# GpSimd makes the angle and decay tables of an S5 block; VectorE keeps the step chain; rotation products are summed in PSUM

## The reference

```python
x_in = x
x = groupnorm(x, groups=32)                 # over 3 channels x 256 positions
u = x.reshape(16, 96, 256).transpose(0, 2, 1)
fx = layernorm(u) * ln1_g + ln1_b           # over the 96 channels
lam = Lambda[:, 0] + 1j * Lambda[:, 1]      # 48 modes
step = exp(log_step)
mask = step * abs(Lambda[:, 1]) / (2 * pi) < 0.25
lam_bar = exp(lam * step)
B_bar = ((lam_bar - 1) / lam)[:, None] * Bc
xs[l] = lam_bar * xs[l-1] + B_bar @ fx[l]   # along the 256 positions
y = 2 * real((Cc * mask) @ xs) + D * fx
y = gelu(y) + fx
fy = layernorm(y) * ln2_g + ln2_b
z1, z2 = split(fy @ W_enc.T)
out = x_in + (z1 * gelu(z2)) @ W_dec.T + fy
```

## Time and profile before

| | us |
|---|---|
| three runs | 110.3, 112.12, 112.47 |
| their median | 112.12 |
| the profiled execution, its own time | 110.42 |
| its span, first to last instruction | 108.6 |
| TensorE matmul busy | 94.9 (87%) |
| VectorE busy | 77.6 (71%) |
| ScalarE busy | 41.0 (38%) |
| GpSimd busy | 31.9 (29%) |

### The profile page before, as it was taken

The page is one execution under the profiler, slowest core; times in us unless marked ns, Lnnn a source line. Parts: engine busy times, 40 slices in busy tenths (PEclk is TensorE's granted clock), DMA queues, the critical chain, the costliest instruction groups (busy, mean ns, idle before and its releaser), DMA issues.

```text
span 108.6 us, 1488 instructions
## 1 busy us (share of the span) xinstructions
PE 94.9 (87%) x502; PEld 56.2 (52%) x502; DVE 77.6 (71%) x260; ACT 41.0 (38%) x79; POOL 31.9 (29%) x26
## 2 busy tenths in 40 slices
PE   5999897269989929999899999999599999999960
PEld 4668766146555715676476655567324432533310
DVE  1688999999986899658677302389990289994590
ACT  2254167807449100024037009818049722024200
POOL 8600000400049992000018000007995000296000
PEclk9999999955799999999999999999999999999997
DMA  2997000000000000000000000000000000450135
GB/s 77 275 262 168 3 0 0 6 0 0 0 0 0 0 0 3 0 6 0 0 0 0 0 0 3 6 0 0 0 0 0 0 0 0 118 149 29 28 84 177
DMA packets 3767, 3.79 MB, mean 35 GB/s; under 512 B 496, under 2 KB 3664, under 8 KB 3760
## 3 DMA queue, kind: packets, MB, share of 16 engines
q1 hardware_dynamic: 3392, 3.49, 12.3%
q10 hardware_dynamic: 368, 0.20, 0.8%
HBM read 2.12 MB, written 1.57 MB: 34 GB/s over the span
## 4 chain that ended last, share of the span: by engine, by line
PE 70%; DVE 21%; issue 4%; ACT 1%; DVEq 1%
PE ps L424 70%; DVE st L836 2%; DVE fy L664 2%; DVE pm L885 2%; DVE sc L694 2%; DVE rs L664 1%; DVE upper L668 1%; DVE sq L664 1%; DVE tb L664 1%; DVE tb L668 1%; DVE y L982 1%; DVE gn L664 1%; DVE rs L694 1%; DVE fx L664 1%; DVE sc L664 1%
## 5 line engine op out<-in xcount | busy, mean ns | idle before, releaser
L424 PE MATMUL ps<-fy,mt 96*96 96x512 f32 x32 | 14.9, 600 | 1.3 <-DVE fy L664 1.3
L290 POOL TENSOR_TENSOR y<-gl,fx 96x512 f32<-96x512 f32 x4 | 6.1, 1524 | 29.8 <-ACT gl L379 29.8
L298 POOL TENSOR_TENSOR res<-fy,xs 96x512 f32<-96x512 f32 x8 | 10.7, 1359 | 11.6 <-DVE fy L664 11.5
L424 PE MATMUL ps<-xs,pm 96*96 96x256 f32 x32 | 10.8, 492 | 3.3 <-DVE pm L885 3.3
L385 ACT ACTIVATE y<-ps,vecs 96x512 f32<-96x512 f32 x8 | 5.5, 687 | 16.4 <-PE ps L424 16.4
L664 DVE SCALAR_TENSOR_TENSOR w<-ps,vecs,y 96x512 f32<-96x512 f32 x8 | 5.9, 743 | 7.4 <-ACT y L385 7.4
L424 PE MATMUL ps<-fx,dm 96*96 96x512 f32 x16 | 8.4, 605 | 2.6 <-issue 2.2
L933 DVE TENSOR_TENSOR Z<-Z,ps 96x240 f32<-96x240 f32 (+3 forms) x8 | 2.8, 355 | 9.5 <-PE ps L424 9.5
L424 PEld LDWEIGHTS ps<-fy,mt 96*96 96x96 f32 x32 | 5.0, 163 | 8.7 <-issue 6.8
L424 PEld LDWEIGHTS ps<-xs,pm 96*96 96x96 f32 x32 | 6.4, 214 | 5.9 <-DVE pm L885 3.8
L379 ACT ACTIVATE gl<-ps,db 96x512 f32<-96x512 f32 x8 | 5.5, 684 | 9.4 <-PE ps L424 9.4
(11 more groups left out here) (112 smaller groups left out, 168.1 us busy)
## 6 DMA issues: line engine op xcount, KB each, us to landing
out_dram<-sq SPq DMA_DIRECT2D x8, 192.0 KB, 2.2
xs<-x_dram SPq DMA_DIRECT2D x3, 384.0 KB, 6.1
xs<-x_dram SPq DMA_DIRECT2D x2, 192.0 KB, 3.5
mt<-mats_dram SPq DMA_DIRECT2D x1, 338.6 KB, 6.8
mt<-mats_dram ACTq DMA_DIRECT2D x1, 180.0 KB, 3.9
sm<-small_dram ACTq DMA_DIRECT2D x1, 8.6 KB, 2.8
cmask<-mask_dram ACTq DMA_DIRECT2D x1, 9.0 KB, 4.9
```

The source lines that it names most:

```text
L290: nc.gpsimd.tensor_tensor(yv[:, RT * i:RT * (i + 1), :], cols(gl, H, i).rearrange("c (b m) -> c b m", b=RT), cols(fx, H, i).rearrange("c ( ...
L298: nc.gpsimd.tensor_tensor(cols(res, H, i), cols(fy, H, i), xs[:, HB * H + 2 * i:HB * H + 2 * i + 2, :].rearrange("c n l -> c (n l)"), ALU. ...
L424: return nc.tensor.matmul(o, lhsT, rhs, start=start, stop=stop)
```

## The change

`parameters()` and `output_tables()` are gone from VectorE. In their place VectorE has `step_chain()`, the part up to TH and RE, which ends in `angle_unit_ready`; it also makes DEN and ABSI. Its steps are laid two behind each statistic of the first half. The order of VectorE between the statistics and the first layernorm is rewritten: no parameter steps stand inside `group_norm` and `inverse_sigma` any more, the statistics of half 1 stand between the `scale_centering` of half 0, and at the end a new `input_bias()` makes the bias column of `bst`.

GpSimd makes everything from ANG and XK on: angle reduction, `expm1_table`, cosine and sines, `bst`, and then the output tables, `db` and `dm`. A step that was one `scalar_tensor_tensor` on VectorE is two instructions there. `rotT` is replaced by `rotC` and `rotS`, both made whole on GpSimd. TensorE multiplies `bst` by both and sums the two in PSUM: four matmuls for two. `yl` is combined before `rotX`. TensorE has fourteen more warm-ups ahead of `center_batch(1, 0)`. The removed functions are left out here, and are in the code above.

```diff
-WARM = (10, 2, 14)
+WARM = (10, 2, 14, 14)
 WARM_N = 256
-FIRST_PM = 4
 ...
+            def expm1_table(p, y, q, arg):
+                settle()
+                ts(y, arg, 1 / 128, -80 / 128, ALU.mult, ALU.max)
+                settle()
+                ts(p, y, 1 / 120, None, ALU.mult)
+                for c in (1 / 24, 1 / 6, 1 / 2, 1.0):
+                    settle()
+                    ts(q, p, c, None, ALU.add)
+                    settle()
+                    tt(p, q, y, ALU.mult)
+                for _ in range(7):
+                    settle()
+                    ts(q, p, 2.0, None, ALU.add)
+                    settle()
+                    tt(p, q, p, ALU.mult)
+            pool.wait_ge(in_small, 16)
+            pool.wait_ge(angle_unit_ready, 2)
+            ts(tbl(ANG), s(KV, NK), scol(TH), None, ALU.mult)
+            ts(tbl(XK), s(KV, NK), scol(RE), None, ALU.mult)
+            settle()
+            ts(tbl(NRND), tbl(ANG), 1 / (2 * np.pi), ROUND, ALU.mult, ALU.add)
+            settle()
+            ts(tbl(NRND), tbl(NRND), -ROUND, None, ALU.add)
+            for part in (TWO_PI_HI, TWO_PI_MID, TWO_PI_LO):
+                settle()
+                ts(tbl(RED), tbl(NRND), -float(part), None, ALU.mult)
+                settle()
+                tt(tbl(ANG), tbl(RED), tbl(ANG), ALU.add)
+            settle()
+            nc.gpsimd.tensor_scalar(tbl(RED), tbl(ANG), PI_BELOW, -PI_BELOW, ALU.min,
+                                    ALU.max).then_inc(angles_ready, 1)
+            expm1_table(tbl(EXM), tbl(TMP), tbl(RK), tbl(XK))
+            pool.wait_ge(sines_ready, 2)
+            tt(tbl(SH2), tbl(SH), tbl(SH), ALU.mult)
+            ts(tbl(NSS), tbl(SIN), s(RHO), None, ALU.mult)
+            settle()
+            ts(tbl(CM1), tbl(SH2), -2.0, None, ALU.mult)
+            ts(tbl(RK), tbl(EXM), 1.0, None, ALU.add)
+            settle()
+            ts(tbl(COS), tbl(CM1), 1.0, None, ALU.add)
+            pool.wait_ge(in_mats, 16)
+            pool.wait_ge(den_ready, 1)
             nc.gpsimd.tensor_tensor(
-                rotT[:, :, :], m(M_ID).unsqueeze(1).broadcast_to([96, T, 96]),
-                tbl(COS, T).unsqueeze(2).broadcast_to([96, T, 96]), ALU.mult).then_inc(rotcos_ready, 1)
-            pool.wait_ge(in_mats, 16)
+                rotS[:, :, :], m(M_SW).unsqueeze(1).broadcast_to([96, T, 96]),
+                tbl(NSS, T).unsqueeze(2).broadcast_to([96, T, 96]), ALU.mult).then_inc(rot_ready, 1)
+            settle()
+            nc.gpsimd.tensor_tensor(
+                rotC[:, :, :], m(M_ID).unsqueeze(1).broadcast_to([96, T, 96]),
+                tbl(COS, T).unsqueeze(2).broadcast_to([96, T, 96]), ALU.mult).then_inc(rot_ready, 1)
+            tt(tbl(RSIN), tbl(RK), tbl(SIN), ALU.mult)
+            tt(scol(T1), tbl(EXM, 1, 1), tbl(COS, 1, 1), ALU.mult)
+            settle()
+            tt(scol(T3), tbl(RSIN, 1, 1), s(LI), ALU.mult)
+            tt(scol(T1), scol(T1), tbl(CM1, 1, 1), ALU.add)
+            settle()
+            tt(scol(T4), scol(T1), s(LI), ALU.mult)
+            ts(scol(CRE), scol(T1), s(LR), scol(T3), ALU.mult, ALU.add)
+            settle()
+            ts(scol(CIM), tbl(RSIN, 1, 1), s(LR), scol(T4), ALU.mult, ALU.subtract)
+            tt(scol(CRE), scol(CRE), scol(DEN), ALU.mult)
+            settle()
+            ts(scol(CIM), scol(CIM), scol(DEN), s(RHO), ALU.mult, ALU.mult)
+            settle()
+            ts(bt1[:, :], m(M_BS), scol(CIM), None, ALU.mult)
+            ts(bst[:, 0:C], m(M_B), scol(CRE), None, ALU.mult)
+            settle()
+            nc.gpsimd.tensor_tensor(bst[:, 0:C], bst[:, 0:C], bt1[:, :], ALU.add).then_inc(bst_ready, 1)
+            ts(tbl(SSG), tbl(SIN), s(NRHO), None, ALU.mult)
+            settle()
+            tt(tbl(RSSG), tbl(RK), tbl(SSG), ALU.mult)
+            settle()
+            tt(scol(ABSI), scol(ABSI), scol(STEP), ALU.mult)
+            settle()
+            ts(scol(MASK), scol(ABSI), float(np.float32(2 * np.pi)) / 4, 2.0, ALU.is_lt, ALU.mult)
+            settle()
+            tt(scol(MR), scol(MASK), s(NRHO), ALU.mult)
+            ts(scol(MI), scol(MASK), -1.0, None, ALU.mult)
+            settle()
+            ts(tbl(CU), tbl(COS), scol(MR), None, ALU.mult)
+            ts(tbl(SU), tbl(SIN), scol(MI), None, ALU.mult)
+            for dst, unit in ((XCO, COS), (XSI, SSG)):
+                ts(tbl(dst, 1, 0), tbl(unit, 1, T), tbl(RK, 1, 1), tbl(RK, 1, 0), ALU.mult, ALU.mult)
+                ts(tbl(dst, 1, 1), tbl(unit, 1, K16), tbl(RK, 1, 1), tbl(RK, 1, T), ALU.mult, ALU.mult)
+                tt(tbl(dst, 4, 2), tbl(unit, 4, K16), tbl(RK, 4, K16), ALU.mult)
+            nc.gpsimd.tensor_tensor(db[:, :], s(DD), s(B1), ALU.mult).then_inc(db_ready, 1)
+            nc.gpsimd.tensor_scalar(dm[:, :], m(M_ID), s(DD), None, ALU.mult).then_inc(dm_ready, 1)
+            settle()
 ...
-            pool.wait_ge(tables_ready, 1)
+            combine(yl, M_C, tbl(CU, T), M_CS, tbl(SU, T), T).then_inc(yl_ready, 1)
             combine(rotX, M_ID, tbl(XCO, NX), M_SW, tbl(XSI, NX), NX).then_inc(rotx_ready, 1)
-            combine(yl, M_C, tbl(CU, T), M_CS, tbl(SU, T), T).then_inc(yl_ready, 1)
 ...
+            warm_up(WARM[3], bank(1, 0))
 ...
             pe.wait_ge(bst_ready, 1)
-            pe.wait_ge(rot_ready, T)
-            mm(bank(0, 2)[0:97, 0:480], bst[:, :], rotT[:, 0:5, :])
-            mm(bank(0, 3)[0:97, 0:288], bst[:, :], rotT[:, 5:8, :]).then_inc(umat_done, 1)
+            pe.wait_ge(bias_col_ready, 1)
+            pe.wait_ge(rot_ready, 2)
+            for part, first, last in ((2, 0, 5), (3, 5, 8)):
+                o = bank(0, part)[0:97, 0:96 * (last - first)]
+                mm(o, bst[:, :], rotS[:, first:last, :], stop=False)
+                last_mm = mm(o, bst[:, :], rotC[:, first:last, :], start=False)
+            last_mm.then_inc(umat_done, 1)
 ...
+            def step_chain():
+                norm.next_stt(scol(REC), s(LS), -1.0, s(LS), ALU.mult, ALU.max)
+                norm.add(nc.vector.tensor_tensor(scol(T2), s(LR), s(LR), ALU.mult))
+                yield
+                norm.next_ts(scol(Y1), scol(REC), 1 / 128, -80 / 128, ALU.mult, ALU.max)
+                norm.add(stt(scol(DEN), s(LI), s(LI), scol(T2), ALU.mult, ALU.add))
+                yield
+                norm.next_ts(scol(EXP), scol(Y1), 1 / 120, None, ALU.mult)
+                nc.vector.reciprocal(scol(DEN), scol(DEN)).then_inc(den_ready, 1)
+                yield
+                for c in (1 / 24, 1 / 6, 1 / 2, 1.0):
+                    norm.next_stt(scol(EXP), scol(EXP), c, scol(Y1), ALU.add, ALU.mult)
+                    yield
+                for _ in range(7):
+                    norm.next_stt(scol(EXP), scol(EXP), 2.0, scol(EXP), ALU.add, ALU.mult)
+                    yield
+                norm.next_ts(scol(EXP1), scol(EXP), 1.0, None, ALU.add)
+                norm.add(scaled(scol(NEG), s(LS), 0.0, None, ALU.is_lt))
+                norm.add(scaled(scol(POS), s(LS), 0.0, None, ALU.is_ge))
+                yield
+                norm.settle()
+                norm.add(nc.vector.reciprocal(scol(REC1), scol(EXP1)))
+                norm.add(stt(scol(ABSI), s(LI), -1.0, s(LI), ALU.mult, ALU.max))
+                yield
+                norm.next_tt(scol(T4), scol(REC1), scol(NEG), ALU.mult)
+                yield
+                norm.next_stt(scol(STEP), scol(EXP1), scol(POS), scol(T4), ALU.mult, ALU.add)
+                yield
+                norm.settle()
+                nc.vector.tensor_tensor(scol(RE), s(LR), scol(STEP), ALU.mult).then_inc(angle_unit_ready, 1)
+                nc.vector.tensor_tensor(scol(TH), s(LI), scol(STEP), ALU.mult).then_inc(angle_unit_ready, 1)
+                yield
+            steps = step_chain()
+            def step_chain_on(count):
+                for _ in range(count):
+                    next(steps, None)
+            def input_bias():
+                dve.wait_ge(bst_ready, 1)
+                norm.add(nc.vector.tensor_tensor(bt1[:, :], bst[:, 0:C], m(M_B1), ALU.mult))
+                norm.settle()
+                nc.vector.reduce_sum(bst[:, C:C + 1], bt1[:, :],
+                                     axis=mybir.AxisListType.X).then_inc(bias_col_ready, 1)
             nc.vector.memset(wm[:, :], 1.0).then_inc(wm_ready, 1)
             dve.wait_ge(in_small, 16)
-            parameter_steps(6)
+            step_chain_on(6)
             for q in range(HB):
                 statistics(0, q)
-                parameter_steps(1)
+                step_chain_on(2)
             dve.wait_ge(in_early, 16)
             statistics(1, 0)
-            group_norm(0, lambda: parameter_steps(1), lambda: (statistics(1, 1), parameter_steps(2)))
+            group_norm(0, lambda j: None, lambda: (statistics(1, 1), statistics(1, 2)))
             for n in range(HB):
                 scale_centering(0, n)
-                if n % 2:
-                    parameter_steps(1)
-            for q in range(2, HB):
```

(44 more changed lines are left out.)

127 lines of the change are left out of this document (14 added, 113 removed).

## The result

The changed kernel took 113.53 us (median of 4 runs, 113.33 to 114.1) against 111.45 us for the kernel before, now over 4 runs: ratio 1.028, 95% interval 1.020 to 1.035. Run again beside the experiments, the same kernel (a0_after) gave 1.015 (1.008 to 1.022). So it is slower, by 1.5 to 2.8%. Some executions of these kernels take longer at a lower TensorE clock; the ratios leave them out, the medians do not, and the ratios of b2, e5 and e6 rest on two executions each. The profiled execution took 113.33 us with a span of 111.5; before, 110.42 and 108.6.

What follows compares the result with a forecast made beforehand. TensorE, with 70% of the chain, was taken as the bound, so moved work counts only where it waits. An earlier `um` (-1.9) and the removed stall (-0.6) gave -2.5 us, from 112.12 to 109.6 us; range 106.0 to 115.0.

Steps and rivals of the forecast that it cites:

- rival C: GpSimd's chain becomes the bound at 0.37 us a stage and TensorE's clock falls: 115 to 117.5 us; chance 0.22.
- VectorE: With most parameter steps gone, `angle_unit_ready` comes near 9.1 and the first `pm` of half 1 near 19.9, against 22.6.
- TensorE up to the product: After fourteen warm-ups, centering keeps the clock up; TensorE is free for the `bst` product near 26.1, against 29.93.
- GpSimd's chain: From `angle_unit_ready` to `bst_ready`: 41 stages at 0.28 us, companions and rotations, 16.3 us plus 0.7 for waits, ending at 26.1.
- The turning point: Rival C decides from about 0.32 us a GpSimd stage, with `bst` at 28.4, where `um` is no earlier than now.
- The clock: In rival C TensorE stands 5.6 us, the product at 1.2 GHz takes up to 5.8 us, `um` at 34.6 to 37.5.
- Behind `um`: TensorE's 2.21 us stall for `yl` goes, but `parts` is late next, so only about 0.6 us is paid out.
- The term of -1.9 us for an earlier `um`: With `bst_ready` at 26.1 on GpSimd, `um` comes at 29.6 instead of 31.46, a gain of 1.9 us.

Runs made afterwards that it cites:

- b2: Kernel before, with sine and cosine halves of the rotations kept apart and their two products summed by TensorE in PSUM: 111.31 us, ratio 0.997.
- e5: Changed kernel with the decay chain back on VectorE and `input_bias` ahead of `inverse_sigma(0, 0)`: ratio 0.966 on two of four executions.
- e6: Changed kernel with 20 warm-ups before TensorE's wait for `bst` and 13 for 10 at the start: 113.61 us, ratio 1.011.
- e1_again: Changed kernel with 26 more warm-ups on TensorE before its wait for `bst`, second measurement: 113.96 us, ratio 1.018.
- e7: As e6, with GpSimd making only the cosine part of `rotX`, one product for three instructions: 111.36 us, ratio 0.994.
- b1_yl_first: Kernel before, with only GpSimd's order changed, `yl` combined before `rotX`: 108.85 us, ratio 0.982.
- e3: Changed kernel without the seven squarings of the decay table on GpSimd, 14 settled instructions fewer: 109.63 us, ratio 0.983.
- e4_split: Changed kernel with the decay table's chain back on VectorE, between steps of group norm 0 and its centering matrices: 112.91 us, ratio 1.007.

## Why the prediction was wrong

It forecast 109.6 us and most chance for faster; its own rival C, GpSimd's chain as the bound with a fallen clock, is what happened, at 0.22. That 113.53 us lies inside the stated range, 106.0 to 115.0, is no merit of the sum: the range is wide enough to hold both signs. Point by point, by its steps.

**VectorE: right.** `angle_unit_ready` was forecast at 9.1 and GpSimd starts at 9.21. The first `pm` of half 1 was forecast at 19.9 and comes at 20.21.

**TensorE up to the product: right.** Free at 26.0 for 26.1, with the clock kept up.

**GpSimd's chain: the step that failed.** 16.3 us were summed, and 0.7 for waits; 20.8 were measured. By parts, from the starts in the timeline (a settled instruction is a stage, one that waits for nothing new a companion):

| part | summed, us | measured, us |
|---|---|---|
| ANG to the start of RED, 9 stages, 1 companion | 2.7 | 3.23 |
| RED and expm1, 24 stages, 1 companion | 6.9 | 8.06 |
| SH2 to COS, 2 stages, 3 companions | 1.1 | 2.00 |
| both rotations | 2.9 | 3.20 |
| RSIN to `bst`, 6 stages, 6 companions | 2.7 | 4.33 |

The stage was taken at 0.28 us; the quiet ones in expm1 take 0.315 (0.63 a pair), all 24 on average 0.33. The text had 0.28 to 0.34 from the arithmetic rows and took the lower end, leaning towards the memset for the one-input instructions. They are not like it: one with constants mostly lasts 0.24 us, more than the 0.21 of a two-input one of the same size. These 33 stages explain 1.7 of the 4.5 us. Most of the rest, 2.5 us, is in the few instructions behind SH2, where every stage was put at 0.28 and every companion at 0.17: those with two per-partition scalars last 0.34, 0.37 and 0.55 us, and the two products of 96x96 with one scalar 0.54 and 0.51 (the second, at 29.05, is not shown above). Waits between the engines explain a part: three instructions take 1.48 us at 21.10, and 0.83 us in e1_again, where VectorE's steps fall elsewhere, and both rotations last 1.64 and 1.63 for 1.47 alone. That is about 1 us, for the 0.7 allowed for the whole chain. That waits are not the main cause is shown by the quiet pairs, which have none in them and follow each other at 0.63 us. The output tables behind `bst` were short in the same way: from `bst` to the first product of `yl` they took 4.7 us (30.03 to 34.76) for 3.4.

**The turning point was in the text.** It said that C decides from 0.32 us a stage. The measured chain is worth 0.315 to 0.34 a stage and 2.5 us more behind SH2, so it lay past that point. The order of the chances was wrong, not the mechanism.

**The clock: mechanism right, price wrong by its cover.** TensorE stood 4.8 us, the clock fell, and the product took 5.3 for 2.6 us. C had `um` at 34.6 to 37.5, and the product was done at 36.2; but it added this delay in full and came to 115 to 117.5. In the changed kernel it costs little: e1_again gave no gain and e6 gave 0.2 to 0.5 us, since the same late GpSimd chain holds `parts` back and broadcast(0, 1) waits for that. e7 shows the other half, by its times: with GpSimd's last product out of the way about 2 us more are paid out. The text also read the clock row one slice late: the clock before is low from the slice at 21.7, not 24.4. Nothing in the sum hangs on it.

**Behind `um`: half right.** The 2.21 us stand did go, and `parts` did become the next to be late (1.17 us in b1_yl_first, 0.63 in e3). What was wrong was to sum from `um`. In the kernel before, neither `um` nor the product set the end of this stage: GpSimd's products, started by VectorE's output tables at 31.47, did, through `yl` and through `parts`. b2_two_products shows it: the product is done about 2 us later in its trace (33.34 for 31.29), and broadcast(0, 1) is the same, and the time within its interval. The term of -1.9 us for an earlier `um` was therefore not there to be had alone; this is concluded from the trace, and no run makes `um` alone earlier. In the changed kernel both chains are late and arrive within 0.1 us of each other: GpSimd's last product ends at 44.73 for 41.50, 3.2 us later, and TensorE's product at 36.2 for 31.5. The better order of the products gave some of it back: broadcast(0, 1) comes 12.5 us after the product, for 14.6 before and 14.0 forecast.

**What stays open.** How much of e4_split's and e5's behaviour is due to the clock at the first warm-ups, which fell in some profiles and not in others, was not tried further. Two more parts of the change were not run alone in the kernel before: the fourteen warm-ups before the centering of half 1, and VectorE's new order of statistics and group norm.

## What to carry to other kernels

Price a chain of small dependent instructions on an engine by the upper bound that its own rows give, and its instructions with per-partition scalars and its wide ones separately: a count of 41 turns 0.05 us into 2 us, most of the gain forecast here. Before an earlier or later event is worth anything, find which chains meet at the next common point and how much slack each has; here two met within 0.1 us, and curing one alone (e6) gave 0.2 to 0.5 us of 2.8. A part of a change can be the gain that the whole hides: reordering two products alone gave 2%.
